# Layer 1 of a two-layer attention kernel: P scaled, split in two 16-bit parts and transposed by DMA; values in two 16-bit parts

## The chip, the cores and the metric

The kernel runs on one core of a Trainium2 chip. A core has TensorE (PE), VectorE (DVE), ScalarE (ACT), GpSimd (POOL) and SyncE (SP), which run side by side, each in its own order, and meet at semaphores; 16 DMA engines move data. The metric is the device time of one execution in microseconds.

## The reference

Two layers on x of shape 2 x 192 x 64 x 64. Layer 0 is an attention of four heads behind a depthwise convolution; the change leaves it alone. Layer 1, cut to what matters:

```python
xf = x.reshape(b, c, h * w).transpose(0, 2, 1)          # group norm before, 4096 tokens, 192 channels
xn = layer_norm(xf) * ln_w + ln_b
Q, K, V = xn @ Wq.T, xn @ Wk.T, xn @ Wv.T
S = einsum('bnd,bmd->bnm', Q, K)                        # 4096 x 4096 an image
attn = e1/(e1+e2) * softmax(S) + e2/(e1+e2) * relu(S)**2
out = einsum('bnm,bmd->bnd', attn, V) + x
```

The second term has no normalisation, so S is squared as it is: that is why products are made from two parts of a value (a rounded high part and the rest).

## The kernel before

`layer1` takes the images one after the other. A prologue per image (group norm, layer norm, projections, stores and loads of q and k) ends with `kst` (keys, two parts), `q_scratch` in HBM and `v_hl`: the values of all 4096 tokens as [high | low], 384 columns, in float32r (F32R), a 4-byte type.

Then comes the attention loop: 32 rows (`RB`) of 128 queries. In a row the 4096 scores stand in 4 chunks of 1024 (`NQ`, index c), two PSUM buffers `ps_s`; P is turned and weighed in 8 groups of 512 keys (`NG`). All five engines have the loop written out by hand as slots: in slot t TensorE makes the scores of row t+1, ScalarE and VectorE finish P of row t, and TensorE weighs row t-1. Odd and even rows use buffer s = 0 or 1.

- TensorE, `score_half` (L1277): five matmuls of 512 columns, half a chunk. `transpose_group` (L1288): four transposes of P into one of three PSUM buffers `ps_t`. `weigh_group` (L1298): four pairs, `at_hi` with 384 columns of `v_hl` and `at_lo` with 192, added up in `ps_o`. `turn_output` (L1307) turns the finished row back to channels by tokens. A score half waits (semaphore `exped`) until ScalarE has read the buffer two chunks before.
- VectorE, `maximum` (L1476, L1478): the chunk's row maximum and the bias of its exp; behind the fourth `nbmin` (L1481). `coefficients` (L1487 to L1493), which wait for ScalarE's `factors`. `combine` (L1500): P = P x coef + square, 128x1024, both inputs in SBUF (`gp` and `vb` or `rn`). `low_group` (L1505): `at_lo` = `ps_t` - `at_hi`, 128x512. `copy_output` (L1510, L1512) and `add_output` (L1519).
- ScalarE, `relu` (L1120), `exp_piece` (L1131), `square` (L1125), `factors` (L1137) and `high_group` (L1143): `at_hi`, the rounded copy of `ps_t`.
- SP issues `load_q`, `load_res` and `store` of a row (L1020, L1025, L1030). GpSimd does nothing in the loop.

In layer 0 GpSimd subtracts too: `lo` = `u` - `hi` (L389), behind VectorE's cast (L641), beside its convolution (L592).

## Time and profile before

| what | value |
|---|---|
| median of 3 runs | 3994.99 us |
| lowest, highest | 3993.24, 3997.37 us |
| the profiled execution | 3993.2 us |
| its span, first to last instruction | 3991.4 us |
| mean granted TensorE clock | 0.957 |
| TensorE, VectorE, ScalarE, GpSimd busy | 3574.1, 2171.5, 2221.6, 342.2 us |

Busy time is a mean over stages with different limits. The attention loops of layer 1 lie at about 2320 to 3060 us (image 0) and 3248 to 3991 us (image 1) of the span; layer 0 ends before 2100. A timeline row gives the start and the length of an instruction or of several of one kind (xN), and in brackets how long the engine had been idle before and what released it. Instructions of one engine overlap by about 0.1 us, so an instruction's share of its engine's time is read from one start to the next. A row of engines by stretch gives the stretch, its length, and each engine's busy time with its number of instructions.

### The profile page before, as it was taken

The numbers are of one execution on the slowest core, as the hardware profiler recorded it, in microseconds if no ns is written. First come the engines' busy times: TensorE is split into PE (matmuls) and PEld (weight loads), VectorE is DVE, ScalarE is ACT, GpSimd is POOL, SyncE is SP. The second block draws the span as 40 slices with busy tenths as digits, with TensorE's granted clock in tenths as the row PEclk, the third lists the DMA queues.
The fourth block names the chain that finished last, engine by engine and source line by source line (L and its number), as shares of the span: only waits on it lengthen the run. The fifth ranks groups of instructions, "written<-read, shape, count | busy, mean of one in ns | idle before, by whom it ended". The sixth has DMA issues, their size and how long they took to land. (4 is left out here: it accounts for less than half of the span.)

```text
span 3991.4 us, 53719 instructions
## 1 busy us (share of the span) xinstructions
PE 3574.1 (90%) x18516; PEld 1946.7 (49%) x18516; DVE 2171.5 (54%) x2749; ACT 2221.6 (56%) x2690; POOL 342.2 (9%) x124
## 2 busy tenths in 40 slices
PE   1269999999999999999997679999998669999999
PEld 0022322223222232222222358888886248888888
DVE  4744157331565234652014457777776447777777
ACT  0036555465555655556661257777773147777776
POOL 0212012020110201101001200000000300000000
PEclk9579999999999999999998889999999789999999
DMA  6221112121121211102003520101012350010100
GB/s 178 55 56 32 40 35 66 36 43 41 33 55 36 50 37 37 50 18 51 3 5 93 162 81 25 29 24 30 24 29 70 107 148 24 25 28 24 30 24 18
DMA packets 166881, 194.73 MB, mean 49 GB/s; under 512 B 28802, under 2 KB 105474, under 8 KB 164994
## 3 DMA queue, kind: packets, MB, share of 16 engines
q1 hardware_dynamic: 166724, 192.65, 18.8%
q8 instruction: 97, 1.59, 0.2%
q14 instruction: 60, 0.49, 0.0%
HBM read 106.01 MB, written 50.92 MB: 39 GB/s over the span
## 5 line engine op out<-in xcount | busy, mean ns | idle before, releaser
L413 ACT ACTIVATE prob<-ps_s,cur 128x1024 f32<-128x1024 f32 x1024 | 1085.5, 1111 | 794.4 <-PE ps_s L493 792.8
L506 PE MATMUL ps_a<-prob,vt 128*64 128x512 f32 x4096 | 997.6, 608 | 0.0
L1277 PE MATMUL ps_s<-kst,qs 128*128 128x512 f32 x2560 | 690.2, 401 | 47.6 <-DMA qs<-q_scratch 34.7
L1298 PE MATMUL ps_o<-v_hl,at_hi 128*128 128x384 f32 x2048 | 646.3, 372 | 2.3 <-DVE at_lo L1505 2.3
L487 PE MATMUL ps_s<-q_a,k_a 128*128 128x512 f16 x2048 | 537.6, 385 | 10.1 <-issue 5.1
L1298 PE MATMUL ps_o<-v_hl,at_lo 128*128 128x192 f32 x2048 | 513.1, 251 | 0.0
L1277 PEld LDWEIGHTS ps_s<-kst,qs 128*128 128x128 f32 x2560 | 448.3, 190 | 120.4 <-issue 37.2
L506 PEld LDWEIGHTS ps_a<-prob,vt 128*64 128x64 f32 x4096 | 249.6, 136 | 412.9 <-issue 412.2
L1505 DVE TENSOR_TENSOR at_lo<-ps_t,at_hi 128x512 fp32r<-128x512 f32 x512 | 351.6, 687 | 155.8 <-ACT at_hi L1143 146.9
L487 PEld LDWEIGHTS ps_s<-q_a,k_a 128*128 128x128 f16 x2048 | 142.9, 98 | 520.5 <-ACT prob L413 412.6
L1476 DVE TENSOR_REDUCE nmx<-ps_s 128x1 f32<-128x1024 f32 x256 | 311.5, 1217 | 153.9 <-PE ps_s L1277 153.9
L1298 PEld LDWEIGHTS ps_o<-v_hl,at_lo 128*128 128x128 f32 x2048 | 391.3, 191 | 4.9
L1298 PEld LDWEIGHTS ps_o<-v_hl,at_hi 128*128 128x128 f32 x2048 | 385.8, 188 | 8.8 <-DVE at_lo L1505 4.0
L1288 PE MATMUL ps_t<-ident,gp 128*128 128x128 f32 x2048 | 299.4, 273 | 22.7 <-DVE at_lo L1505 22.7
L1143 ACT ACTIVATE at_hi<-ps_t 128x512 fp32r<-128x512 f32 x512 | 294.1, 603 | 28.5 <-PE ps_t L1288 28.5
L1131 ACT ACTIVATE gp<-ps_s,nbias,mix 128x1024 f32<-128x1024 f32 x256 | 308.7, 1206 | 0.0
L666 DVE RECIPROCAL rden<-ps_h 128x512 f32<-128x512 f32 x32 | 107.5, 3358 | 340.6 <-PE ps_h L461 340.6
L592 DVE SCALAR_TENSOR_TENSOR qk<-pad,vec,qk 112x2048 f32<-112x2048 f32 x128 | 290.3, 2346 | 0.0
L1288 PEld LDWEIGHTS ps_t<-ident,gp 128*128 128x128 f32 x2048 | 241.5, 140 | 78.1 <-issue 32.4
L575 DVE TENSOR_SCALAR pad<-ps_h,vec 112x512 f32<-112x512 f32 x96 | 72.2, 752 | 333.7 <-PE ps_h L430 333.7
L1120 ACT ACTIVATE vb<-ps_s 128x1024 f32<-128x1024 f32 x128 | 131.4, 1027 | 217.3 <-DVE nmx L1476 217.3
L1120 ACT ACTIVATE rn<-ps_s 128x1024 f32<-128x1024 f32 x128 | 131.4, 1027 | 184.3 <-DVE nmx L1476 184.3
(143 smaller groups left out, 2902.9 us busy)
## 6 DMA issues: line engine op xcount, KB each, us to landing
z<-z_scratch SPq DMA_DIRECT2D x96, 384.0 KB, 3.6
q_scratch<-qst SPq DMA_DIRECT2D x64, 384.0 KB, 5.0
qs<-q_scratch SPq DMA_DIRECT2D x64, 384.0 KB, 3.8
sq<-rn_scratch SPq DMA_DIRECT2D x16, 768.0 KB, 10.2
gn_x<-in_x SPq DMA_DIRECT2D x4, 1536.0 KB, 18.4
z_scratch<-gn_x SPq DMA_DIRECT2D x4, 1536.0 KB, 11.6
q_a<-hi SPq DMA_DIRECT2D x64, 96.0 KB, 2.3
o_scratch<-o_s SPq DMA_DIRECT2D x64, 96.0 KB, 1.9
```

Source lines behind the costliest of these rows:

```text
L413: act.activation(prob[:, a % PR, :], ps_s[:, a % 2, :], ACT.Exp, bias=cur[:, slot:slot + 1], scale=1.0 / SPLIT).then_inc(exped, 1)
L487: pe.matmul(ps_s[:, n % 2, h * CH:(h + 1) * CH], k_a[:, slot, m * P:(m + 1) * P], q_a[:, slot, cols], start=True, stop=False)
L506: ins = pe.matmul(ps_a[h * HALF:(h + 1) * HALF, j % 2, :], vt[:, slot, m, :], prob[:, a % PR, h * CH:(h + 1) * CH], start=(m == 0), stop=( ...
L592: ins = dve.scalar_tensor_tensor(out=out, in0=src, scalar=vec[0:KR, slot, 1 + tap:2 + tap], in1=out, op0=ALU.mult, op1=ALU.add)
L1120: act.activation(sqr[s][:, cols], ps_s[:, c % 2, :], ACT.Relu).then_inc(relued, 1)
L1131: act.activation(prob[s][:, c * QB:(c + 1) * QB], ps_s[:, c % 2, :], ACT.Exp, bias=nbias[:, s, c:c + 1], scale=mix[:, 6:7], accum_out=sums ...
L1143: act.activation(at_hi[:, j % 4, :], ps_t[:, turn_bank(at), :], ACT.Copy).then_inc(hi_made, 1)
L1277: ins = pe.matmul(ps_s[:, c % 2, h * CH:(h + 1) * CH], qs[:, s, qt, :], kst[:, ktile, cols], start=(t == 0), stop=(t == len(terms) - 1))
L1288: ins = pe.transpose(ps_t[:, turn_bank(at), m * P:(m + 1) * P], prob[s][:, cols], ident[:, :])
L1298: ins = pe.matmul(ps_o[:, 0:wide], a[:, j % 4, m * P:(m + 1) * P], v_hl[:, kt, 0:wide], start=(kt == 0 and t == 0), stop=(kt == KT - 1 and ...
L1476: dve.tensor_reduce(nmx[:, c:c + 1], ps_s[:, c % 2, :], AX_X, ALU.max, negate=True).then_inc(mx_op, 1)
L1505: dve.tensor_tensor(at_lo[:, j % 4, :], ps_t[:, turn_bank(at), :], at_hi[:, j % 4, :].bitcast(F32), ALU.subtract).then_inc(t_free, 1)
```

## The change

P is scaled by powers that keep it inside the 16-bit range: relu by `GAIN`, square by `inv` (one over the row's largest score, at least one), the coefficients by the same factor, and the output by `back` and per channel by `unscale`. `v_hl`, scaled by `scale_v` through `wv`, is F16. A few instructions before the first image (`reach_step`) work out `scale_v` and `unscale`.

P's high part is no longer made from a transposed copy in PSUM. VectorE casts each combined chunk to `p_hi` (`high`, F16), GpSimd subtracts to `p_lo` (`lows`), and SP issues one DMA transpose for each part and chunk (`turn_chunk`), eight a row, into `at_hi` and `at_lo`, which now hold a whole row twice. ScalarE's `high_group`, VectorE's `low_group` and TensorE's `transpose_group` are gone. SP's loop is written out without a hardware loop.

```diff
-        v_hl = sb("v_hl", [P, KT, 2 * C], F32R)
+        v_hl = sb("v_hl", [P, KT, 2 * C], F16)
-        at_hi = sb("at_hi", [P, 4, GR * P], F32R)
-        at_lo = sb("at_lo", [P, 4, GR * P], F32R)
+        at_hi = sb("at_hi", [P, 2, KT, P], F16)
+        at_lo = sb("at_lo", [P, 2, KT, P], F16)
+        p_hi = sb("p_hi", [P, N], F16)
+        p_lo = sb("p_lo", [P, N], F16)
...
+                    def turn_chunk(row, s, c, first=False):
+                        cols = slice(c * QB, (c + 1) * QB)
+                        if not first:
+                            sp.wait_ge(w_done, NG * (RB * b + row - 2) + 2 * c + 2)
+                        sp.wait_ge(hi_made, NQ * (RB * b + row) + c + 1)
+                        sp.dma_start_transpose(at_hi[:, s, c * KC:(c + 1) * KC, :], p_hi[:, cols]).then_inc(turned[c], 16)
+                        sp.wait_ge(lo_made, NQ * (RB * b + row) + c + 1)
+                        sp.dma_start_transpose(at_lo[:, s, c * KC:(c + 1) * KC, :], p_lo[:, cols]).then_inc(turned[c], 16)
+
+                    def slot(t, s, first=False, more_q=True):
+                        for c in range(NQ):
+                            turn_chunk(t, s, c, first and t < 2 and b == 0)
+                            if c == 0:
+                                if more_q:
+                                    load_q(t + 2, s)
+                                if not first:
+                                    store(t - 2, s)
+                                load_res(t, s, first and b == 0)
...
+                    def lows(row, s):
+                        for c in range(NQ):
+                            cols = slice(c * QB, (c + 1) * QB)
+                            pool.wait_ge(hi_made, NQ * (RB * b + row) + c + 1)
+                            pool.tensor_tensor(p_lo[:, cols], prob[s][:, cols], p_hi[:, cols], ALU.subtract).then_inc(lo_made, 1)
+
+                    with pool.Fori(0, RB // 2) as r:
+                        lows(2 * r, 0)
+                        lows(2 * r + 1, 1)
...
-                        act.activation(sqr[s][:, cols], ps_s[:, c % 2, :], ACT.Relu).then_inc(relued, 1)
+                        act.activation(sqr[s][:, cols], ps_s[:, c % 2, :], ACT.Relu, scale=GAIN).then_inc(relued, 1)
-                        act.activation(sqr[s][:, cols], sqr[s][:, cols], ACT.Square).then_inc(squared, 1)
-
+                        act.activation(sqr[s][:, cols], sqr[s][:, cols], ACT.Square, scale=inv[:, s:s + 1]).then_inc(squared, 1)
+
+                    def exp_piece(row, s, c, first=False):
                         act.wait_ge(mx_op, MX * (RB * b + row) + 2 * c + 2)
-                        if at is not None:
-                            act.wait_ge(t_full, turn(b, row - 2, at) + 1)
+                        if not first:
+                            act.wait_ge(lo_made, NQ * (RB * b + row - 2) + c + 1)
...
+                    def slot(t, s, new=True, first=False, older=False):
+
+                        exp_piece(t, s, NQ - 1, older)
+                        factors(t, s)
+                        square(t, s, 0)
+                        square(t, s, 1)
+                        if new:
+                            relu(t + 1, 1 - s, 0, first)
+                        square(t, s, 2)
+                        if new:
+                            exp_piece(t + 1, 1 - s, 0, first)
+                        square(t, s, 3)
+                        if new:
+                            for c in range(1, NQ):
+                                relu(t + 1, 1 - s, c, first)
+                                if c < NQ - 1:
+                                    exp_piece(t + 1, 1 - s, c, first)
...
-                    def transpose_group(row, s, j, at):
-                        pe.wait_ge(t_free, turn(b, row, at) + 1)
-                        if j % 2 == 0:
-                            pe.wait_ge(p_made, NQ * (RB * b + row) + j // 2 + 1)
+                    def weigh_group(row, s, u, first=False):
+                        if u == 0 and not first:
+                            pe.wait_ge(ob_made, RB * b + row - 1)
+                        if u % 2 == 0:
+                            pe.wait_ge(turned[u // 2], 32 * (RB * b + row + 1))
                         for m in range(GR):
-                            cols = slice((j * GR + m) * P, (j * GR + m + 1) * P)
-                            ins = pe.transpose(ps_t[:, turn_bank(at), m * P:(m + 1) * P], prob[s][:, cols], ident[:, :])
-                        ins.then_inc(t_full, 1)
-
-                    def weigh_group(row, j, at):
-                        pe.wait_ge(t_free, TR + turn(b, row, at) + 1)
-                        if j == 0:
-                            pe.wait_ge(ob_made, RB * b + row + 1)
-                        for m in range(GR):
-                            kt = j * GR + m
+                            kt = u * GR + m
                             for t, (a, wide) in enumerate(((at_hi, 2 * C), (at_lo, C))):
-                                ins = pe.matmul(ps_o[:, 0:wide], a[:, j % 4, m * P:(m + 1) * P], v_hl[:, kt, 0:wide],
+                                ins = pe.matmul(ps_o[:, s * CH:s * CH + wide], a[:, s, kt, :], v_hl[:, kt, 0:wide],
                                                 start=(kt == 0 and t == 0), stop=(kt == KT - 1 and t == 1))
                         ins.then_inc(w_done, 1)
...
-                    def slot(t, s, j, q, new):
-
-                        for g in range(2):
-                            transpose_group(t - 1, 1 - s, g, place(q, g))
+                    def slot(t, s, j, new=True, out=True, first=False):
+
                         for u in range(NG):
                             if new:
                                 score_half(t + 1, 1 - s, j, u)
-                            if u == 0 and q >= 1:
-                                turn_output(t - 2, 2)
-                            if u + 2 < NG:
-                                transpose_group(t - 1, 1 - s, u + 2, place(q, u + 2))
-                            weigh_group(t - 1, u, place(q, u))
+                            if u == 1 and out:
+                                turn_output(t - 2, s, first)
+                            weigh_group(t - 1, 1 - s, u, first)
...
+                reach_step(dve.scalar_tensor_tensor(out=g[:, :, 0:C], in0=wv[:, :, :], scalar=-1.0, in1=wv[:, :, :],
+                                                    op0=ALU.mult, op1=ALU.max))
+                for t in range(CT):
+                    reach_step(dve.tensor_scalar(g[:, t, 0:C], g[:, t, 0:C], reach[:, t, 2:3], None, ALU.mult))
+                dve.wait_ge(reach_full, 1)
+                reach_step(dve.tensor_scalar(scale_v[:, :], ps_t[0:CP, 0, 0:C], 1e-30, C / SPAN, ALU.max, ALU.mult))
...
+                for t in range(CT):
+                    dve.tensor_tensor(wv[:, t, :], wv[:, t, :], scale_v[:, :], ALU.mult)
+                    ins = dve.tensor_scalar(unscale[:, t:t + 1], ps_t[0:CP, 1, t * 8:t * 8 + 1], 1e-30, C / SPAN, ALU.max, ALU.mult)
+                reach_step(ins)
...
+                            dve.wait_ge(mx_op, at + 2 * NQ + 1)
+                            dve.tensor_scalar(m1[:, s:s + 1], nbmin[:, s:s + 1], mix[:, 7:8], -1.0, ALU.mult, ALU.min).then_inc(mx_op, 1)
+                            dve.wait_ge(mx_op, at + 2 * NQ + 2)
+                            dve.reciprocal(inv[:, s:s + 1], m1[:, s:s + 1]).then_inc(mx_op, 1)
...
+                        dve.scalar_tensor_tensor(out=back[:, s:s + 1], in0=m1[:, s:s + 1], scalar=1.0 / (GAIN * GAIN),
+                                                 in1=m1[:, s:s + 1], op0=ALU.mult, op1=ALU.mult).then_inc(c_op, 1)
+                        dve.wait_ge(c_op, at + 3)
+                        dve.tensor_tensor(total[:, :], total[:, :], back[:, s:s + 1], ALU.mult).then_inc(c_op, 1)
+                        dve.wait_ge(c_op, at + 4)
                         dve.reciprocal(total[:, :], total[:, :]).then_inc(c_op, 1)
-                        dve.wait_ge(c_op, at + 3)
+                        dve.wait_ge(c_op, at + 5)
                         dve.tensor_scalar(coef[:, s, :], fac[:, s, :], total[:, 0:1], mix[:, 4:5], ALU.mult, ALU.mult).then_inc(c_op, 1)
-                        dve.wait_ge(c_op, at + 4)
+                        dve.wait_ge(c_op, at + 6)
...
-                    def low_group(row, j, at):
-                        dve.wait_ge(hi_made, NG * (RB * b + row) + j + 1)
-                        dve.tensor_tensor(at_lo[:, j % 4, :], ps_t[:, turn_bank(at), :], at_hi[:, j % 4, :].bitcast(F32),
-                                          ALU.subtract).then_inc(t_free, 1)
+                    def high(row, s, c, first=False):
+
+                        cols = slice(c * QB, (c + 1) * QB)
+                        dve.wait_ge(p_made, NQ * (RB * b + row) + c + 1)
+                        if not first:
+                            dve.wait_ge(turned[c], 32 * (RB * b + row))
+                        dve.tensor_copy(p_hi[:, cols], prob[s][:, cols]).then_inc(hi_made, 1)
+                    def copy_output(row, s):
+                        dve.wait_ge(w_done, NG * (RB * b + row) + NG)
+                        dve.tensor_scalar(ob_lo[:, :], ps_o[:, s * CH + C:s * CH + 2 * C], back[:, s:s + 1], None,
+                                          ALU.mult).then_inc(ob_lo_made, 1)
-                        dve.tensor_tensor(ob[:, :], ps_o[:, 0:C], ob_lo[:, :], ALU.add).then_inc(ob_made, 1)
+                        dve.scalar_tensor_tensor(out=ob[:, :], in0=ps_o[:, s * CH:s * CH + C], scalar=back[:, s:s + 1],
+                                                 in1=ob_lo[:, :], op0=ALU.mult, op1=ALU.add).then_inc(ob_made, 1)
...
-                        dve.tensor_tensor(ot[:, s, :, :], ps_t[0:CP, turn_bank(at), 0:CT * P].rearrange("p (t n) -> p t n", t=CT),
-                                          res[:, s, :, :], ALU.add).then_inc(t_free, 1)
+                        for t in range(CT):
+                            ins = dve.scalar_tensor_tensor(out=ot[:, s, t, :], in0=ps_t[0:CP, s, t * P:(t + 1) * P],
+                                                           scalar=unscale[:, t:t + 1], in1=res[:, s, t, :],
+                                                           op0=ALU.mult, op1=ALU.add)
+                        ins.then_inc(ot_made, 1)
+
+                    def slot(t, s, j, new=True, out=True, first=False):
+
+                        if out:
+                            copy_output(t - 2, s)
+                        coefficients(t, s)
+                        combine(t, s, 0)
+                        high(t, s, 0, first)
+                        if out:
+                            add_output(t - 2, s, j)
                         if new:
                             maximum(t + 1, 1 - s, 0)
-                        if old:
-                            combine(t, s, 1)
-                        low(3)
-                        if old:
-                            combine(t, s, 2)
-                        low(4)
+                        combine(t, s, 1)
+                        high(t, s, 1, first)
                         if new:
                             maximum(t + 1, 1 - s, 1)
-                        if old:
-                            combine(t, s, 3)
-                        low(5)
-                        low(6)
+                        combine(t, s, 2)
+                        high(t, s, 2, first)
+                        combine(t, s, 3)
+                        high(t, s, 3, first)
                         if new:
                             maximum(t + 1, 1 - s, 2)
-                        low(7)
-                        if new:
                             maximum(t + 1, 1 - s, 3)
```

TensorE, image 0, one step of the loop with a new row to score: scores of one half, the turn of P, a weigh group. Before:

```order
L1277 MATMUL ps_s<-kst,qs 128x512 x5
L1288 MATMUL ps_t<-ident,gp 128x128 x4
L1298 MATMUL ps_o<-v_hl,at_hi 128x384
L1298 MATMUL ps_o<-v_hl,at_lo 128x192
L1298 MATMUL ps_o<-v_hl,at_hi 128x384
L1298 MATMUL ps_o<-v_hl,at_lo 128x192
L1298 MATMUL ps_o<-v_hl,at_hi 128x384
```

After:

```order
L1287 MATMUL ps_s<-kst,qs 128x512 x5
L1300 MATMUL ps_o<-v_hl,at_hi 128x384
L1300 MATMUL ps_o<-v_hl,at_lo 128x192
L1300 MATMUL ps_o<-v_hl,at_hi 128x384
L1300 MATMUL ps_o<-v_hl,at_lo 128x192
L1300 MATMUL ps_o<-v_hl,at_hi 128x384
```

The four transposes of a step have gone; scores and weigh groups stand in the same order and number.

VectorE, the middle of an early row (combines, maxima, and before the low parts; `gp` is P, `rn` the square). Before:

```order
L1500 SCALAR_TENSOR_TENSOR gp<-gp,coef,rn 128x1024 [waits squared]
L1505 TENSOR_TENSOR at_lo<-ps_t,at_hi 128x512 [waits hi_made]
L1500 SCALAR_TENSOR_TENSOR gp<-gp,coef,rn 128x1024 [waits squared]
L1505 TENSOR_TENSOR at_lo<-ps_t,at_hi 128x512 [waits hi_made]
L1476 TENSOR_REDUCE nmx<-ps_s 128x1 [waits s_full]
L1478 TENSOR_SCALAR nbias<-nmx,mix 128x1 [waits mx_op]
L1500 SCALAR_TENSOR_TENSOR gp<-gp,coef,rn 128x1024 [waits squared]
L1505 TENSOR_TENSOR at_lo<-ps_t,at_hi 128x512 [waits hi_made] x2
L1476 TENSOR_REDUCE nmx<-ps_s 128x1 [waits s_full]
L1478 TENSOR_SCALAR nbias<-nmx,mix 128x1 [waits mx_op]
L1505 TENSOR_TENSOR at_lo<-ps_t,at_hi 128x512 [waits hi_made]
```

After:

```order
L1531 SCALAR_TENSOR_TENSOR gp<-gp,coef,rn 128x1024 [waits squared]
L1540 CAST p_hi<-gp 128x1024 [waits turned1,p_made]
L1499 TENSOR_REDUCE nmx<-ps_s 128x1 [waits s_full]
L1501 TENSOR_SCALAR nbias<-nmx,mix 128x1 [waits mx_op]
L1531 SCALAR_TENSOR_TENSOR gp<-gp,coef,rn 128x1024 [waits squared]
L1540 CAST p_hi<-gp 128x1024 [waits turned2,p_made]
L1531 SCALAR_TENSOR_TENSOR gp<-gp,coef,rn 128x1024 [waits squared]
L1540 CAST p_hi<-gp 128x1024 [waits turned3,p_made]
L1499 TENSOR_REDUCE nmx<-ps_s 128x1 [waits s_full]
L1501 TENSOR_SCALAR nbias<-nmx,mix 128x1 [waits mx_op]
L1499 TENSOR_REDUCE nmx<-ps_s 128x1 [waits s_full]
L1501 TENSOR_SCALAR nbias<-nmx,mix 128x1 [waits mx_op]
```

Each combine is now followed by a cast to `p_hi`, combines 2 and 3 stand together, and the maxima of chunks 2 and 3 have moved behind them to the row's end.

SP, the last rows of an image before, and one row of image 0 after. Before:

```order
L1020 DMA qs<-q_scratch 128x6x128 [waits s_full]
L1025 DMA res<-res_scratch 96x2x128 [waits ot_stored]
L1030 DMA out<-ot 96x2x128 [waits t_free]
L1025 DMA res<-res_scratch 96x2x128 [waits ot_out,ot_stored]
L1030 DMA out<-ot 96x2x128 [waits t_free]
```

After:

```order
L1042 DMA_TRANSPOSE at_hi<-p_hi 128x8x128 [waits hi_made,w_done]
L1044 DMA_TRANSPOSE at_lo<-p_lo 128x8x128 [waits lo_made1]
L1023 DMA qs<-q_scratch 128x6x128 [waits s_full]
L1034 DMA out<-ot 96x2x128 [waits ot_made]
L1029 DMA res<-res_scratch 96x2x128 [waits ot_made]
L1042 DMA_TRANSPOSE at_hi<-p_hi 128x8x128 [waits hi_made,w_done]
L1044 DMA_TRANSPOSE at_lo<-p_lo 128x8x128 [waits lo_made1]
```

The load of qs, the store and the load of res stand behind the first chunk's two transposes, and six more transposes follow.

## Rows read from the trace of the kernel before

**Rows 1.** engines by stretch: PE, PEld, DVE, ACT, POOL busy us, clock, DMA share, GB/s
```profile
2700.00:2926.00 226.00, 222.67 (x1382) 200.35 (x1381) 174.11 (x282) 167.32 (x251) 0.00 (x0) 1.00 0.09 26
```

**Rows 2.** timeline of SP's queue: start, us, instruction; stores of two rows
```profile
2423.74 0.34 SPq L1030 DMA_DIRECT2D out<-ot  x1
...
2446.35 0.34 SPq L1030 DMA_DIRECT2D out<-ot  x1
```

**Rows 3.** timeline of TensorE, one step of a row
```profile
2408.25 1.33 PE L1277 MATMUL ps_s<-kst,qs 128*128 128x512 f32 x5
2409.41 0.60 PE L1288 MATMUL ps_t<-ident,gp 128*128 128x128 f32 x4
2409.77 0.42 PE L1298 MATMUL ps_o<-v_hl,at_hi 128*128 128x384 f32 x1
...
2410.97 1.33 PE L1277 MATMUL ps_s<-kst,qs 128*128 128x512 f32 x5
```

**Rows 4.** timeline of VectorE in the same row
```profile
2419.44 0.36 DVE L1510 COPY ob_lo<-ps_o 128x192 f32<-128x192 f32 x1 [0.40 <-issue]
...
2421.55 0.16 DVE L1487 TENSOR_TENSOR part<-fac,sums 128x4 f32<-128x4 f32 x1 [0.68 <-ACT fac L1137]
...
2422.55 0.69 DVE L1505 TENSOR_TENSOR at_lo<-ps_t,at_hi 128x512 fp32r<-128x512 f32 x1
...
2425.29 1.21 DVE L1476 TENSOR_REDUCE nmx<-ps_s 128x1 f32<-128x1024 f32 x1
...
2426.67 1.27 DVE L1500 SCALAR_TENSOR_TENSOR gp<-gp,coef,vb 128x1024 f32<-128x1024 f32 x1
```

**Rows 5.** timeline, layer 0: cast, VectorE beside GpSimd
```profile
646.58 0.69 DVE L641 CAST hi<-u 112x1024 f16<-112x1024 f32 x1
...
647.19 8.75 DVE L592 SCALAR_TENSOR_TENSOR vv<-pad,vec,vv 112x2048 f32<-112x2048 f32 x3
...
647.36 4.17 POOL L389 TENSOR_TENSOR lo<-u,hi 112x1024 f16<-112x1024 f32 x1 [7.58 <-DVE hi L641]
```

**Rows 6.** timeline of ScalarE: relu, exp, factors
```profile
2418.64 1.03 ACT L1120 ACTIVATE vb<-ps_s 128x1024 f32<-128x1024 f32 x1 [0.53 <-DVE nmx L1476]
...
2420.03 1.21 ACT L1131 ACTIVATE gp<-ps_s,nbias,mix 128x1024 f32<-128x1024 f32 x1
...
2421.22 0.30 ACT L1137 ACTIVATE fac<-nbias,nbmin 128x4 f32<-128x4 f32 x1
```

**Rows 7.** one line's instructions: ns min/median/max
```profile
L389 POOL TENSOR_TENSOR lo<-u,hi x32: 2127/3148/4183, 191.2 to 1853.1; 112x1024 f16<-112x1024 f32 x32
```

**Rows 8.** timeline, layer 1 before the loop: two-element mode beside GpSimd
```profile
2236.30 0.87 DVE L1467 TENSOR_SCALAR gp<-gp,pvec 96x512 f32<-96x512 f32 x2
...
2238.34 2.36 POOL L1076 TENSOR_TENSOR xs<-gp,xs 96x1024 fp32r<-96x1024 f32 x1 [14.40 <-ACT xs L1095]
...
2238.42 2.96 DVE L1467 TENSOR_SCALAR gp<-gp,pvec 96x512 f32<-96x512 f32 x2
```

**Rows 9.** timeline, layer 1 before the loop: an operand in PSUM beside GpSimd
```profile
3179.98 2.35 POOL L1076 TENSOR_TENSOR xs<-gp,xs 96x1024 fp32r<-96x1024 f32 x1 [6.79 <-ACT xs L1095]
3180.92 1.22 DVE L1450 TENSOR_TENSOR qst<-ps_s,qst 96x1024 fp32r<-96x1024 f32 x1 [2.10 <-ACT qst L1102]
```

**Rows 10.** timeline, layer 0's start: a copy of one column beside GpSimd
```profile
71.42 1.65 POOL L393 TENSOR_TENSOR root<-root,half_t 128x8 f32<-128x8 f32 x1 [0.32 <-DVE root L679]
71.59 0.15 DVE L655 COPY cur<-tabs 128x1 f32<-128x1 f32 x1
```

**Rows 11.** timeline: TensorE's first score of image 0, SP's first load of image 1
```profile
2320.65 6.89 PE L1277 MATMUL ps_s<-kst,qs 128*128 128x512 f32 x20 [18.85 <-DMA qs<-q_scratch]
...
3061.76 0.32 SPq L971 DMA_DIRECT2D o_buf<-o_scratch  x1
```

**Rows 12.** timeline of TensorE, image 1's run-up: after an idle
```profile
3271.54 7.57 PE L1277 MATMUL ps_s<-kst,qs 128*128 128x512 f32 x20 [3.24 <-ACT gp L1131]
```

**Rows 13.** engines by stretch, columns as in Rows 1: 2 us of that run-up
```profile
3272.00:3274.00 2.00, 2.00 (x6) 1.52 (x6) 1.97 (x3) 1.39 (x3) 0.00 (x0) 0.50 0.00 0
```

225 lines of the change are left out of this document (95 added, 130 removed).

## The prediction, made before the changed kernel ran

> **What bounds the kernel now.** The change touches layer 1 alone, in its attention loop, so I read that stage. The table of engines by stretch [rows 1], over ten of its rows, has TensorE busy 222.67 of 226 us at the full granted clock; VectorE has 174.11, ScalarE 167.32, GpSimd nothing, and the DMA engines are 9% busy. TensorE is the bound. Two successive stores of one row's output are 22.61 us apart [rows 2]; that is the period of a row, 32 to an image. The order of TensorE's work inside a row shows where it goes [rows 3]: a score half (five matmuls) holds it from 2408.25 to 2409.41 = 1.16 us, four transposes of P to 2409.77 = 0.36, four pairs of P x V to 2410.97 = 1.20, so 2.72 a step. Eight steps make 21.8; the output's turn and a short wait at the row's end are the rest.
>
> **TensorE after.** The 32 transposes go: 8 x 0.36 = 2.9 us. P x V keeps its columns (576 a pair), now in 16 bits. A pair took about 0.29; 576 columns at 2.4 GHz are 0.24. So a group costs 0.96 to 1.15, and I take 1.0. A row then needs 8 x (1.16 + 1.0) + 0.3 = 17.6 us: TensorE alone would give 5 us a row. The rest of this working asks what is late next.
>
> **VectorE's own work after**, as start-to-start times in today's rows [rows 4]:
> - output copy 0.36 (2419.44) and sum, as long again: 0.74 from start to start;
> - the coefficients: today 2421.55 to 2422.55 = 1.00, with two more tiny instructions of 0.17 = 1.34;
> - four maxima with their bias: 2425.29 to 2426.67 = 1.38 each, 5.5; plus nbmin, m1 and inv behind the last, 0.7;
> - four combines at 1.27, each now followed by a cast that waits for it, so 1.30 each, 5.2;
> - four casts f32 to f16. Layer 0 has the same instruction on 112 partitions: 0.69, and 0.61 from start to start [rows 5]; 2.4 together;
> - the output sum, now in two pieces: 0.45.
> Together 16.4. The eight low parts (0.60 each, 4.8) are gone; that is what pays for casts and small steps. ScalarE loses eight copies of P and needs relu (1.03), exp with its read (2420.03 to 2421.22 = 1.19) and a square like the relu, four times each: about 12.6 [rows 6]. Neither engine's sum reaches 17.6.
>
> **The wait for ScalarE.** In the new order VectorE does the maxima 2 and 3 back to back at the end of a row. From the end of maximum 2, ScalarE has relu, exp, relu, exp and the factors before it: 2 x (1.03 + 1.19) + 0.3, less 0.2 where one starts before the last is through = 4.5 us [rows 6]. VectorE has bias, maximum 3, its small steps and the output copy: 1.4 + 0.7 + 0.74 + 0.1 = 2.95. So it stands about 1.6 before the coefficients. Queued behind that wait is the whole of its row.
>
> **GpSimd and the lock.** The low part of P moves to GpSimd: four subtractions of 128x1024 a row. Layer 0 has this form (f16 from f32 and f16); the shortest took 2127 ns [rows 7]. The same place shows what it does beside VectorE [rows 5]: the subtraction asked for at 647.36 took 4.17, because a VectorE instruction with two SBUF inputs had started at 647.19 (2.35 alone); and three of those took 8.75, where 3 x 2.26 = 6.8 was due, so one of them stood 1.9. Whichever starts first keeps the other out to its end. A single-input instruction that runs at two elements a cycle is shut out too: two of L1467 take 0.87 (2236.30); the next two, at 2238.42, took 2.96, since a GpSimd subtraction had started at 2238.34 [rows 8]. VectorE instructions that read PSUM are not: L1450 took its usual 1.22 inside a GpSimd subtraction [rows 9]. So combines and casts are locked out, maxima and output steps are not.
>
> Now the row in its new order. Cast 0 starts low 0 (2.13); VectorE has the output sum and maximum 0 (1.8) to do, then combine 1 stands 0.35. Cast 1 starts low 1; only maximum 1 (1.38) lies beside it: combine 2 stands 0.8. Behind cast 2 comes combine 3 at once; as in layer 0 it starts before the semaphore reaches GpSimd, low 2 waits for it, and cast 3 then stands a whole 2.13. Low 3 lies beside maxima 2 and 3 and the output copy: nothing. Together 3.3 us. **Sum: 16.4 + 1.6 + 3.3 + 0.3 (loop branches and single waits, 0.15 today) = 21.6 us a row**, against 22.61. TensorE waits 4 us of it.
>
> Small instructions of one element per partition I take as free of the lock: a copy of 128x1 at 71.59 took 0.15 while GpSimd ran from 71.42 for 1.65 [rows 10]. The Trainium skill (SBUF — State Buffer, practical consequences) says that copies and tensor_scalar can all enter the two-port modes and contend; by it the bias of maximum 2 would stand 1 us behind low 3, and rival B below is that case.
>
> **The transposes by DMA.** No row shows one. Eight a row, 256 KB each, 2 MB in all. Today's traffic of a row (qs, res and out, 576 KB in 1152 pieces of 512 B, 72 per engine) keeps an engine 0.09 x 22.6 = 2.0 us busy [rows 1], 28 ns a piece. A transpose of 128x1024 cut at its 128-column blocks has 1024 pieces of 256 B, 64 per engine: 14 ns each if bytes count, 28 if pieces do, so 0.9 to 1.8 us. Nearest in kind is the piece; I take 1.4. With today's 2.0 a row needs 9 to 16.5 us of the DMA engines, hidden under 21.6. Its latency is hidden too: chunk 0 of a row is needed 15 us after its cast, and at_hi and at_lo have two slots. The lower bound of its cost is therefore nothing. SP's queue has eight transposes with two semaphores each; behind them stand the load of qs (needed 13 us later), the store and the load of res. It holds while one transpose costs SP or the DMA engines under (21.6 - 1.5) / 8 = 2.5 us.
>
> The Trainium skill gives two prices. DMA: Bandwidth & Descriptors (Latency and other measured facts) has 261 GB/s for transposes, an estimate of 1.0 us each. The same page (on HWDGE) has 262,144 sequencer cycles for 8,192 tiles in earlier generations, 32 a tile; at the SyncEngine's 1.2 GHz (Trainium Kernel Development and Optimization) 64 tiles would hold SP 1.7 us, 14 us a row as an estimate. No row here shows either; by both the sum stays as it is.
>
> **The whole.** An image's attention lasts from its first score at 2320.65 to the next image's first load at 3061.76, 741.1 us [rows 11]: 31 periods of 22.6 and 40.5 of run-up and run-off. After: 31 x 21.6 + 39 = 708.6, since the last row now passes a transpose but loses the copies. That is 32.5 less, 65 for both images. The new steps on wv before the first chunk lie mostly beside loads; 2 us. **3993.2 - 63 = 3930 us**, for a profiled execution that stood 1.8 under the median, so the same number serves for the median.
>
> **Rivals.**
> - **B, small steps are locked too.** Then the bias of maximum 2 stands 1 us behind low 3 and the row takes 22.2: 31 x 22.2 + 39 = 727, 27 less for both images, 3968; a little more overhead and it is 3990, no change.
> - **C, the casts escape the lock.** For: L1467 is one case. Then lows 0 to 2 fit behind maxima, VectorE's row is its 16.4 plus waits for exp and scores, 19.9 in all: 31 x 19.9 + 30 = 647, 3805.
> - **D, the transposes bound** (slower). From 2.5 us a transpose, in SP's queue or the DMA engines, they set the row; every 0.1 us adds 0.8. At 3.0 the row is 24 + 1.5 = 25.5: 31 x 25.5 + 45 = 836, 95 more an image, 4183. For: a write of 16 rows' elements is far finer than any row shows. Against: 2.5 us for 64 pieces an engine is 39 ns, above the 28 of twice the size.
> - **E, the clock falls** (slower). TensorE would idle 2.3 us at a row's end and 1.5 in its middle. After an idle of 3.24 us, before 3271.54 [rows 12], the clock stood at 0.50, 1.2 GHz [rows 13]. If it fell so at every row, the first two steps would take twice as long, maximum 0 would wait, and the row be 23.3: 761 an image, 4035. The idle is shorter than the one that did it.
> - **The change isn't made**: the instruction order shows DMA_TRANSPOSE and no TensorE transpose of P, so this has no share.
>
> **Chances.** Forecast (own range 3895 to 3960) 0.53; B 0.12; C 0.11; D 0.14; E 0.10. Faster by over 0.2% (3987; about what a measurement of this kernel tells from no change): forecast, C and half of B, with a small loss to the edges, 0.68. Within 0.2%: the other half of B and the mild end of D, 0.08. Slower: 0.24. The range takes in C and E, and leaves out D's upper part and what lies below C: 3800 to 4045.
>
> **What would show it.** Right: row period 21 to 22; VectorE gaps of about 2 us before a cast with GpSimd busy; GpSimd subtractions of 2.1 and some of 3.4; TensorE busy about 80% of the stage at 1.00. Wrong: subtractions never above 2.2 and no standing casts (C); SP's transposes back to back and P x V waiting for them (D); a granted clock below 0.9 in the stage (E); nbias at over 1 us (B).

## Result: 3896 us, 2.5% faster, and the profile after

The changed kernel takes 3895.98 us (median; 3895.58 to 3897.90) against 3996.09 (3993.24 to 3997.37): a ratio of 0.9751, 95% interval 0.9734 to 0.9768. The forecast was 3930 us, two thirds of the gain. The measured time lies inside the stated range (3800 to 4045 us) and at the lower edge of the forecast's own (3895 to 3960).

Engines over the stretch of [rows 1], same columns:

```profile
2700.00:2926.00 226.00, 194.91 (x1143) 134.23 (x1142) 200.97 (x314) 141.46 (x187) 102.64 (x43) 1.00 0.64 130
```

TensorE is down from 222.67 to 194.91 us of 226, VectorE is up from 174.11 to 200.97, GpSimd does 102.64 where it did nothing, and the DMA share went from 0.09 to 0.64. The clock is 1.00. The chain that ended last, as shares of the span, now runs through VectorE's combinations (L1531) and maxima (L1499):

```profile
DVE 22%; issue 9%; PE 5%; ACT 4%; SPq 2%; POOL 2%; DMA 1%; DVEq 0%; ACTq 0%; POOLq 0%
DVE gp L1531 10%; DVE nmx L1499 7%; ACT gp L1155 3%; PE ps_s L1233 2%; DVE p_hi L1540 1%; SPq L1009 1%; SPq L1000 1%; POOL xg L1085 1%; DVE ot L1557 1%; PE ps_s L1287 1%; PE ps_o L1300 1%; PE ps_s L1254 1%; DVE coef L1524 0%; DMA rn<-r_scratch 0%; DMA q_scratch<-qst 0%
```

TensorE in that stretch (start, us). A step has lost its transposes [rows 3]:

```profile
2602.54 1.39 PE L1287 MATMUL ps_s<-kst,qs 128*128 128x512 f32 x5
2603.78 0.34 PE L1300 MATMUL ps_o<-v_hl,at_hi 128*128 128x384 f16 x1
...
2604.72 1.39 PE L1287 MATMUL ps_s<-kst,qs 128*128 128x512 f32 x5
...
2608.39 1.43 PE L1287 MATMUL ps_s<-kst,qs 128*128 128x512 f32 x5 [1.28 <-ACT gp L1155]
...
2619.01 1.43 PE L1287 MATMUL ps_s<-kst,qs 128*128 128x512 f32 x5 [1.47 <-ACT gp L1155]
```

From score half to score half it is 2604.72 - 2602.54 = 2.18 us (was 2.72), and twice a row TensorE now stands, 1.28 and 1.47 us, until ScalarE's exponential has freed a score bank. It is no longer the bound. VectorE and GpSimd over a row (start, us; in brackets the idle time before it and what ended it):

```profile
2606.05 0.21 DVE L1501 TENSOR_SCALAR nbias<-nmx,mix 128x1 f32<-128x1 f32 x1
...
2610.66 0.16 DVE L1514 TENSOR_TENSOR part<-fac,sums 128x4 f32<-128x4 f32 x1 [1.56 <-ACT fac L1161]
...
2611.92 1.28 DVE L1531 SCALAR_TENSOR_TENSOR gp<-gp,coef,rn 128x1024 f32<-128x1024 f32 x1
2613.33 0.69 DVE L1540 CAST p_hi<-gp 128x1024 f16<-128x1024 f32 x1
...
2615.84 1.48 DVE L1531 SCALAR_TENSOR_TENSOR gp<-gp,coef,rn 128x1024 f32<-128x1024 f32 x1
...
2619.35 2.00 DVE L1531 SCALAR_TENSOR_TENSOR gp<-gp,coef,rn 128x1024 f32<-128x1024 f32 x1
2621.39 0.69 DVE L1540 CAST p_hi<-gp 128x1024 f16<-128x1024 f32 x1
2622.00 1.28 DVE L1531 SCALAR_TENSOR_TENSOR gp<-gp,coef,rn 128x1024 f32<-128x1024 f32 x1
2623.31 2.52 DVE L1540 CAST p_hi<-gp 128x1024 f16<-128x1024 f32 x1
...
2629.58 0.42 DVE L1544 TENSOR_SCALAR ob_lo<-ps_o,back 128x192 f32<-128x192 f32 x1 [0.35 <-issue]
...
2631.52 0.16 DVE L1514 TENSOR_TENSOR part<-fac,sums 128x4 f32<-128x4 f32 x1 [1.07 <-ACT fac L1161]
```

```profile
2604.97 2.14 POOL L1097 TENSOR_TENSOR p_lo<-gp,p_hi 128x1024 f16<-128x1024 f32 x1 [0.63 <-DVE p_hi L1540]
...
2618.13 2.14 POOL L1097 TENSOR_TENSOR p_lo<-gp,p_hi 128x1024 f16<-128x1024 f32 x1 [1.89 <-DVE p_hi L1540]
2622.16 3.11 POOL L1097 TENSOR_TENSOR p_lo<-gp,p_hi 128x1024 f16<-128x1024 f32 x1 [1.89 <-DVE p_hi L1540]
```

The combination takes 1.27 alone and the cast 0.69. The combination at 2615.84 took 1.48, the one at 2619.35 2.00, the cast at 2623.31 2.52: each has a GpSimd subtraction beside it and ends after it. Below, such an instruction is said to stand. GpSimd's subtraction at 2622.16 took 3.11 in place of 2.13, since the combination of 2622.00 was first. In the next row VectorE is idle in two pieces, 0.35 us with no other engine to release it and 1.07 for ScalarE's factors; the two kinds of row take turns (20.86 and 20.99 us). The DMA transposes, on SyncE's queue (ns min/median/max) with their time to landing:

```profile
L1042 SPq DMA_TRANSPOSE at_hi<-p_hi x256: 1230/1282/1957, 2340.7 to 3880.8; - x128
...
DMA to landing us min/median/max: 3.1/3.3/5.6
```

### The profile page after: what moved, and what is told of

Its sections match the earlier page's. It is cut to its first block and busy times, and to the rows that moved or that the text cites. A ratio compares the mean times of both kernels' runs of the same rounds, so it can differ in the third digit from the quotient of the medians.

```text
span 3894.2 us, 48213 instructions
## 1 busy us (share of the span) xinstructions
PE 3310.9 (85%) x16480; PEld 1472.9 (38%) x16480; DVE 2261.5 (58%) x2824; ACT 1979.0 (51%) x2178; POOL 956.6 (25%) x380
## 5 line engine op out<-in xcount | busy, mean ns | idle before, releaser
L1287 PE MATMUL ps_s<-kst,qs 128*128 128x512 f32 x2560 | 722.3, 414 | 221.8 <-ACT gp L1155 186.9
L1097 POOL TENSOR_TENSOR p_lo<-gp,p_hi 128x1024 f16<-128x1024 f32 x256 | 614.5, 2400 | 803.4 <-DVE p_hi L1540 803.4
L1300 PE MATMUL ps_o<-v_hl,at_hi 128*128 128x384 f16 x2048 | 552.8, 331 | 8.5 <-DMA at_lo<-p_lo 8.5
L1300 PE MATMUL ps_o<-v_hl,at_lo 128*128 128x192 f16 x2048 | 506.0, 248 | 0.0
L1499 DVE TENSOR_REDUCE nmx<-ps_s 128x1 f32<-128x1024 f32 x256 | 310.7, 1214 | 48.8 <-PE ps_s L1287 48.8
L1540 DVE CAST p_hi<-gp 128x1024 f16<-128x1024 f32 x256 | 301.4, 1177 | 13.7
L390 POOL TENSOR_TENSOR sq<-qk 112x1024 f32<-112x1024 f32 x32 | 59.6, 1894 | 992.8 <-DVE qk L598 992.8
L1300 PEld LDWEIGHTS ps_o<-v_hl,at_hi 128*128 128x128 f16 x2048 | 201.0, 98 | 228.0 <-issue 129.0
L436 PE MATMUL ps_h<-z,w 96*112 96x512 f32 x384 | 186.8, 620 | 39.4 <-DMA z<-z_scratch 39.3
L499 PE MATMUL ps_s<-q_b,k_b 16*128 16x512 f16 x2048 | 203.5, 387 | 0.0
```

Source lines behind the costliest of these rows:

```text
L1097: pool.tensor_tensor(p_lo[:, cols], prob[s][:, cols], p_hi[:, cols], ALU.subtract).then_inc(lo_made, 1)
L1287: ins = pe.matmul(ps_s[:, c % 2, h * CH:(h + 1) * CH], qs[:, s, qt, :], kst[:, ktile, cols], start=(t == 0), stop=(t == len(terms) - 1))
L1300: ins = pe.matmul(ps_o[:, s * CH:s * CH + wide], a[:, s, kt, :], v_hl[:, kt, 0:wide], start=(kt == 0 and t == 0), stop=(kt == KT - 1 and t ...
L1499: dve.tensor_reduce(nmx[:, c:c + 1], ps_s[:, c % 2, :], AX_X, ALU.max, negate=True).then_inc(mx_op, 1)
L1540: dve.tensor_copy(p_hi[:, cols], prob[s][:, cols]).then_inc(hi_made, 1)
```

## The experiments

Theory A, from the profile: a row is now VectorE's: about 16.6 us of its own, 1.3 of waiting for ScalarE's factors (1.56 at 2610.66, 1.07 at 2631.52), 0.2 for the gap of 0.35 in every second row, and 2.8 in which GpSimd's subtractions keep it out. The expectations below have 16.4 and 1.56 in place of 16.6 and 1.3; they took the longer wait for both rows. Theory B: it is still TensorE's. Theory C: it is set by the transposes, on SyncE's queue or the DMA engines. "Row" in this table is the time from the first to the last row's coefficients in image 0, divided by 31. In the kernel before, that mean takes in a first row of 16.2 us; its steady row is 22.59 us (22.55 and 22.63 in turn), that of the kernel after 20.92. The kernels that leave work out are marked * (half_lows half of the low parts, the others the last product of a score).

| kernel | row, us | time, us | ratio to before (95%) |
|---|---|---|---|
| before | 22.37 | 3996 | 1 |
| after | 20.95 | 3896 | 0.9751 (0.9734 to 0.9768) |
| half_lows * | 20.37 | 3857 | 0.9659 (0.9643 to 0.9675) |
| twice_lows | 24.98 | 4162 | 1.0414 (1.0397 to 1.0432) |
| max2_early | 20.45 | 3864 | 0.9675 (0.9658 to 0.9691) |
| max0_early | 23.84 | 4084 | 1.0225 (1.0208 to 1.0242) |
| both_early | 20.35 (image 1: 21.20) | 3896 | 0.9753 (0.9737 to 0.9769) |
| max2_fill | 20.05 | 3844 | 0.9626 (0.9613 to 0.9639) |
| best_order | 17.51 | 3693 | 0.9245 (0.9230 to 0.9260) |
| four_terms * | 20.89 | 3893 | 0.9749 (0.9733 to 0.9766) |
| best_four * | 16.71 | 3642 | 0.9110 (0.9095 to 0.9126) |
| before_four * | 21.70 | 3950 | 0.9889 (0.9872 to 0.9905) |
| turn12 | 21.19 | 3916 | 0.9803 (0.9787 to 0.9819) |
| best_turn12 | 18.56 | 3770 | 0.9435 (0.9419 to 0.9451) |

### How much GpSimd's work costs VectorE: half_lows and twice_lows

```diff
@@ lows, half_lows
-                            cols = slice(c * QB, (c + 1) * QB)
+                            cols = slice(c * QB, c * QB + CH)
@@ lows, twice_lows
+                            pool.tensor_tensor(p_lo[:, cols], prob[s][:, cols], p_hi[:, cols], ALU.subtract).then_inc(lo_once, 1)
+                            pool.wait_ge(lo_once, NQ * (RB * b + row) + c + 1)
                             pool.tensor_tensor(p_lo[:, cols], prob[s][:, cols], p_hi[:, cols], ALU.subtract).then_inc(lo_made, 1)
```

half_lows also clears `p_lo` once, before the first image; the low parts that are not formed stay zero.

> Leaves out: GpSimd forms the low part of half the columns only (128x512 per chunk in place of 128x1024; the other half of the low part stays zero), so each of its four subtractions a row should fall from 2.13 to about 1.05 us. Theory A (the row is VectorE's: its own 16.4 us, 1.56 us of waiting for ScalarE's factors and 2.75 us in which VectorE and GpSimd keep each other out): the stalls fall by half or more, the row goes from 20.92 to 19.5 us (19.1 to 20.0), the kernel from 3896 to about 3808 us (3785 to 3840). Theory B (TensorE still sets the row, 86% busy) and theory C (the transposes by DMA or SyncE's queue set it, which are the same eight as before): row and kernel stay, 3885 to 3900 us.

> The kernel after the change with each of GpSimd's subtractions made twice in a row (8 x 2.13 us a row in place of 4; the result is the same). Theory A: VectorE is kept out twice as often: of its four pairs of combination and cast each meets a subtraction that runs, the stalls go from 2.75 us a row to 7 to 9 us, the row from 20.92 to 23.5 to 27.5 us, most likely 26, the kernel to 4210 us (4055 to 4305). Rival (GpSimd's busy time, 8.5 of 20.9 us before the doubling and 17 after, is felt only through the low parts' later arrival, a row ahead of their use): 3896 to 3910 us.

Measured: 3857 us, 17 above the expected range, and 4162 us, inside it. B and C, and the rival for twice_lows, are out: the row follows GpSimd's work although nothing waits long for the low parts. Doubling gives 4.0 us a row, where I took 5 for likeliest. VectorE in twice_lows, from the middle of one row to the middle of the next:

```profile
2599.86 2.00 DVE L1534 SCALAR_TENSOR_TENSOR gp<-gp,coef,vb 128x1024 f32<-128x1024 f32 x1
2601.90 2.52 DVE L1543 CAST p_hi<-gp 128x1024 f16<-128x1024 f32 x1
2604.34 1.27 DVE L1534 SCALAR_TENSOR_TENSOR gp<-gp,coef,vb 128x1024 f32<-128x1024 f32 x1
2605.64 2.50 DVE L1543 CAST p_hi<-gp 128x1024 f16<-128x1024 f32 x1
...
2613.92 0.53 DVE L1517 TENSOR_TENSOR part<-fac,sums 128x4 f32<-128x4 f32 x1 [1.56 <-ACT fac L1164]
...
2621.16 2.52 DVE L1543 CAST p_hi<-gp 128x1024 f16<-128x1024 f32 x1
```

GpSimd's:

```profile
2600.86 3.00 POOL L1100 TENSOR_TENSOR p_lo<-gp,p_hi 128x1024 f16<-128x1024 f32 x1
...
2612.28 2.14 POOL L1100 TENSOR_TENSOR p_lo<-gp,p_hi 128x1024 f16<-128x1024 f32 x1
```

Casts 1, 2 and 3 stand 1.8 us each, combination 2 0.7 and the first instruction of the coefficients 0.4: 6.6 us a row in place of 2.8, and the difference is nearly the whole of the row's 4.0.

Halving gave 0.6 us a row, where I expected 1.4. Of VectorE's stands one of 0.8 us is left there (cast 3), and another wait appears. TensorE, half_lows:

```profile
2609.01 1.42 PE L1290 MATMUL ps_s<-kst,qs 128*128 128x512 f32 x5 [2.25 <-ACT gp L1158]
```

and VectorE waits 1.70 us, to 2616.99, for the scores behind them before its last maximum. VectorE and TensorE stand in a ring: exponential 0 frees the bank for the scores of chunk 2, then come chunk 3's, maximum 3, the factors, the coefficients, combination 0, cast 0, maximum 0, and exponential 0 of the next row. With most of the stalls out, a steady row takes 20.0 to 20.3 us; five of them take 21.5 to 21.7, and each of the five has a stretch of TensorE at half its granted clock (of this more under max2_fill), which makes the mean of 20.4. That the ring is what holds the other rows at 20 was argued from the order of the waits here; best_order, which opens it, tests it. The prediction left it out.

### Which work stands beside the subtraction: max2_early, max0_early, both_early

The same instructions in another order on VectorE, nothing else:

```diff
@@ vector engine's slot, max2_early
                         high(t, s, 2, first)
+                        if new:
+                            maximum(t + 1, 1 - s, 2)
                         combine(t, s, 3)
                         high(t, s, 3, first)
                         if new:
-                            maximum(t + 1, 1 - s, 2)
                             maximum(t + 1, 1 - s, 3)
@@ max0_early (both_early is the two together)
                             copy_output(t - 2, s)
+                        if new:
+                            maximum(t + 1, 1 - s, 0)
                         coefficients(t, s)
...
-                        if new:
-                            maximum(t + 1, 1 - s, 0)
                         combine(t, s, 1)
```

> Same work in another order on VectorE alone: the maximum over chunk 2 of the next row stands between cast 2 and combination 3, no longer behind cast 3. Theory A: GpSimd's subtraction of chunk 2 then runs beside a maximum, which reads PSUM and isn't kept out; cast 3 loses its stall of 1.83 us, the row falls from 20.92 to about 19.6 us (19.1 to 20.2), the kernel to about 3815 us (3785 to 3850). Theory B and C: nothing that TensorE or the transposes do changes, and each finds its input at most 1.4 us earlier or later; 3880 to 3905 us.

> Same work in another order on VectorE alone: the maximum over chunk 0 of the next row stands ahead of the coefficients, where VectorE waits 1.56 us a row for ScalarE, and no longer between cast 0 and combination 1. Theory A: the wait is filled (1.4 us gained), but now combination 1 and cast 1 stand right behind cast 0, where GpSimd's subtraction runs: up to 2.13 us of stall for combination 1 in place of 0.20 us, and every later cast then is behind a subtraction that came late. The row gets longer, 22 to 24.3 us, the kernel 3965 to 4105 us, most likely 4060. Rival A2 (VectorE sets the row, but the stalls with GpSimd are no part of it: it would wait for the squares at these places anyway): the row falls by the filled wait to about 19.4 us, 3800 us. Theories B and C: 3880 to 3905 us.

> Same work: maximum 0 ahead of the coefficients, as in the run that took 4084 us, and maximum 2 between cast 2 and combination 3, as in the run that took 3864 us. Theory A (stalls with GpSimd follow from which work stands behind a cast): with maximum 2 back between, cast 3 and combination 3 lose most of their stall, but combination 1 and cast 1 still stand right behind cast 0 (one cast of 2.5 us a row): row 19.3 to 20.8 us, most likely 20.0, kernel 3840 us (3795 to 3890). Rival (effects of the two moves add): 3896 + 188 - 32 = 4052 us.

Measured: 3864 us (14 above the expected range), 4084 (inside it) and 3896 (6 above it, 56 above the likeliest value). Moving one maximum into a wait made the kernel 4.8% slower, as A said and A2, B and C did not. VectorE in max0_early:

```profile
2601.27 1.23 DVE L1499 TENSOR_REDUCE nmx<-ps_s 128x1 f32<-128x1024 f32 x1 [2.94 <-PE ps_s L1287]
...
2606.45 1.27 DVE L1531 SCALAR_TENSOR_TENSOR gp<-gp,coef,rn 128x1024 f32<-128x1024 f32 x1
2607.76 2.52 DVE L1540 CAST p_hi<-gp 128x1024 f16<-128x1024 f32 x1
...
2611.57 1.98 DVE L1531 SCALAR_TENSOR_TENSOR gp<-gp,coef,rn 128x1024 f32<-128x1024 f32 x1
...
2615.51 2.50 DVE L1540 CAST p_hi<-gp 128x1024 f16<-128x1024 f32 x1
```

Cast 1 and cast 3 both take 2.5 us, 1.8 more than alone: no maximum lies beside the subtraction before them. The place is the one that A named, but I had put the stall on combination 1, which started first and stood for nothing; it is cast 1 behind it that stands. That makes 1.8 + 0.7 + 1.8 = 4.3 us a row in place of 2.8. The wait that the move was to fill came back as 2.94 us for TensorE's scores (in the next row 2.44 and a gap of 0.36): 16.6 + 4.3 + 2.9 = 23.8, the measured row. TensorE's own wait, and the engines by stretch right behind it (columns as in [rows 1]):

```profile
2613.71 1.45 PE L1287 MATMUL ps_s<-kst,qs 128*128 128x512 f32 x5 [2.58 <-ACT gp L1155]
```

```profile
2615.00:2619.00 4.00, 4.00 (x16) 2.64 (x16) 3.97 (x3) 0.00 (x0) 3.37 (x2) 0.57 1.08 203
```

After an idle of 2.58 us the granted clock is 0.57 over four microseconds: 1.2 GHz for most of them. Nearly every row of image 0 has such a stretch, and the mean over the image is 0.92. How much of the 2.94 us that makes was not separated. max2_early shows the cast cured (2616.70, 2620.72: 0.69 each) and the ring again at 20.4; here too the clock fell in one row, after a wait of 2.33 us (2634.48), and not in the one before, after 2.25 (2614.31). The next fall of that image came after a wait of 2.25 (2736.54), with waits of 2.33 before it that left the clock at 1.00.

In both_early, image 0 has a row of 20.35, near the 20.0 that I expected, and image 1 one of 21.20 (657.3 us over 31 rows) with a mean clock of 0.96 in place of 0.99. TensorE's wait and the stretch behind it there:

```profile
3635.90 1.43 PE L1287 MATMUL ps_s<-kst,qs 128*128 128x512 f32 x5 [2.61 <-ACT gp L1155]
```

```profile
3637.00:3641.00 4.00, 4.00 (x16) 2.55 (x15) 3.35 (x4) 2.21 (x3) 2.11 (x2) 0.57 1.09 205
```

After a wait of 2.61 us the clock was down; in image 0 the waits are 2.39 and 2.47, and it stayed at 1.00 there. But the length of the wait doesn't settle it: image 1 goes in threes, with a fall after 2.61 and after 2.58 us and none after the longest:

```profile
3594.82 1.43 PE L1287 MATMUL ps_s<-kst,qs 128*128 128x512 f32 x5 [2.78 <-ACT gp L1155]
```

Why the two images differ is open.

### What the clock costs: max2_fill

```diff
@@ score_half, max2_fill: on top of max2_early
+                        if u == 4:
+                            for i in range(8):
+                                pe.matmul(ps_t[:, s, CH // 2:CH], qs[:, s, i % 3, :], kst[:, i % 3, 0:CH // 2], start=True, stop=True)
                         if h == 0:
```

> The order that took 3864 us (maximum 2 early), with eight matmuls of 256 columns added to TensorE's row right ahead of its wait for exponential 0, into columns of PSUM that nobody reads: some 0.9 us that lie in a wait of 2.3 us. In that order the granted clock is 0.98 over the attention stages; it is 0.50 for some 3.7 us after the wait of 2.33 us ending at 2634.48 and stays 1.00 after the one of 2.25 us ending at 2614.31. Theory (the falls of the clock cost part of the row): the wait is shorter, the clock stays at 1.00, and the row of 20.45 us loses the 0.2 to 0.5 us that the falls add: kernel 3845 us (3832 to 3856), with more work on TensorE. Rival (the falls lie inside TensorE's slack and cost nothing; or the added work delays the ring): 3860 to 3890 us.

Measured: 3844.44 us (3838.82 to 3845.95), 20 us less than max2_early (3861.59 to 3870.36), with more work on TensorE. Its wait and image 0 as a whole, after and then before the filler:

```profile
2603.49 1.20 PE L1280 MATMUL ps_t<-kst,qs 128*128 128x256 f32 x8
2605.97 1.42 PE L1290 MATMUL ps_s<-kst,qs 128*128 128x512 f32 x5 [1.28 <-ACT gp L1155]
```

```profile
2340.00:2960.00 620.00, 574.34 (x3465) 411.86 (x3465) 526.47 (x890) 403.65 (x527) 265.16 (x124) 1.00 0.67 134
```

```profile
2340.00:2960.00 620.00, 547.17 (x3157) 381.48 (x3156) 515.57 (x877) 395.22 (x515) 258.76 (x121) 0.98 0.65 130
```

The wait is 1.28 us in place of 2.25, the clock 1.00 in place of 0.98, the row 20.05 in place of 20.45. The falls did cost part of the row; what is left, 20.05 us, is what the ring holds with the clock at full speed.

### TensorE: four_terms, before_four, best_four

```diff
@@ score_half, in each of the three
-                        terms = [(0, 0), (3, 0), (1, 1), (4, 1), (2, 2)]
+                        terms = [(0, 0), (3, 0), (1, 1), (4, 1)]
```

> Leaves out: the last of the five products that make up a score (the low by low one), so each half of a score takes four matmuls in place of five: 0.23 us less eight times a row, 1.84 us of TensorE a row. Theory B (TensorE sets the row): the row falls from 20.92 to 19.1 us, the kernel to 3782 us plus what the edges give (3770 to 3800). Theory A: TensorE has 2.9 us idle a row already; the scores come a little earlier, the row falls by at most 0.3 us, 3875 to 3897 us. Theory C: no change, 3890 to 3900 us.

> The kernel before, without the last of the five products of a score (0.23 us less eight times a row, 1.84 us of TensorE): what relief of TensorE alone is worth in the old loop. If TensorE alone set its row of 22.61 us, 20.8 us and 3994 - 114 = 3880 us. Its VectorE is nearly as long (it copies half of the transposed groups out of PSUM too), so I expect part of that only: 21.4 us (20.8 to 22.2), kernel 3920 us (3880 to 3970). Rival (the old row was never TensorE's): 3990 us.

> The order of the 3693 us run without the fifth product of a score (1.84 us of TensorE a row less), which gave 3 us in the loop whose row took 20.9. Theory: in this order TensorE sets the row (busy 400.00 of 400 us in the second image), VectorE is next with 16.4 us of its own and 0.6 us of stalls: the row falls from 17.5 to 16.6 to 17.4 us, the kernel to 3665 us (3635 to 3688). Rival (VectorE and TensorE are bound by one another in a ring, as in the other orders): 3688 to 3695 us.

Taking 1.84 us a row off TensorE is worth 0.06 us in the kernel after (3 us in all), 0.67 in the kernel before, 0.81 in the order of the next section. So B is out for the kernel after, and the forecast's first step, that TensorE bounds the kernel before, was true for the first 0.7 us only (steady row 22.59 to 21.91). In before_four TensorE is busy

```profile
2700.00:2926.00 226.00, 213.84 (x1339) 189.24 (x1339) 178.38 (x293) 173.04 (x262) 0.00 (x0) 1.00 0.09 26
```

95%, and it waits for VectorE's low parts of P, 18.5 us in 400 where it was 6.0. The bound behind it stood 3% away. By this run a change that only took work off TensorE would have gained little; this one also took the eight low parts of 0.60 us off VectorE.

### The transposes: turn12 and best_turn12

```diff
@@ turn_chunk, turn12: each high part once more, to a spare tile
                         sp.dma_start_transpose(at_hi[:, s, c * KC:(c + 1) * KC, :], p_hi[:, cols]).then_inc(turned[c], 16)
-                        sp.wait_ge(lo_made, NQ * (RB * b + row) + c + 1)
+                        n = NQ * (RB * b + row) + c
+                        if n:
+                            sp.wait_ge(x_in, 16 * n)
+                        sp.dma_start_transpose(at_x[:, :, :], p_hi[:, cols]).then_inc(x_in, 16)
+                        sp.wait_ge(lo_made, n + 1)
@@ high
                             dve.wait_ge(turned[c], 32 * (RB * b + row))
+                            dve.wait_ge(x_in, 16 * (NQ * (RB * b + row - 1) + c + 1))
```

Both also make room for the spare tile, by letting two weights of the prologue (`wq`, `wk`) share their place with later tiles. best_turn12 is the same edit on best_order.

> Adds four transposes by DMA a row: each high part is transposed a second time, to a spare tile that nobody reads (12 in place of 8). Theory A: the DMA engines' share goes from 13.4 to 19.1 us of a row of 20.9, SyncE's queue from some 12 to 18 us, both still under the row: the low parts' transposes start up to 1.4 us later, which TensorE, a row behind, doesn't feel: 3890 to 3912 us. Theory C (transposes or their queue already set the row): 4 x 1.35 us more a row, 26 us, 4200 us or more.

> The order of the 3693 us run, whose row takes 17.5 us, with the four transposes a row that nobody reads added (12 in place of 8; they cost 20 us in all in the loop whose row took 20.9 us). From that run the DMA engines are busy 88% of 21.2 us = 18.7 us a row with twelve transposes. Theory: the transposes come to set the row here, because 18.7 us is over 17.5: 18.7 to 19.6 us a row, kernel 3693 + 62 x 1.2 to 2.1 = 3767 to 3823 us, most likely 3785. Rival (the DMA engines' share is no bound of its own, latency is all that counts and is hidden by a whole row): 3693 to 3725 us, the 20 us of before at most.

turn12: 3916 us, 0.24 us a row more, 4 us past what I allowed. C (4200) is out. VectorE's queue is enough to explain the rest: from combination 0 to cast 0 it is 1.50 us for 1.41 (2611.92 to 2613.33) with one more semaphore wait ahead of the cast. There are four a row, and the last takes its 0.09 out of cast 3's stand (2.43 for 2.52), which leaves 0.27. best_turn12: 3770 us, in the range of the theory. Both as a whole over their image 0:

```profile
2340.00:2980.00 640.00, 543.28 (x3141) 374.45 (x3140) 558.32 (x871) 390.03 (x512) 288.16 (x121) 0.99 0.90 176
```

```profile
2340.00:2900.00 560.00, 529.05 (x3129) 369.49 (x3130) 487.36 (x866) 395.90 (x512) 344.27 (x120) 1.00 1.01 198
```

In the second the DMA engines are busy all the time (1.01), and TensorE waits for the load of the next row's qs, 25 us in this stretch: the transposes set the row. SyncE's queue is full too, though. Two loads of qs in it:

```profile
2609.77 0.58 SPq L1026 DMA_DIRECT2D qs<-q_scratch  x1
...
2628.27 0.58 SPq L1026 DMA_DIRECT2D qs<-q_scratch  x1
```

In these 18.50 us stand twelve transposes and two more DMAs with gaps of at most 0.1 us. Whether the engines or the queue decides was not separated. A transpose costs the DMA engines (0.90 x 21.19 - 0.64 x 20.95) / 4 = 1.4 us, and (1.01 x 18.56 - 0.77 x 17.51) / 4 = 1.3 by the other pair. So rival D's mechanism exists; with eight transposes the DMA engines would decide in a row shorter than 8 x 1.4 + 2 = 13 us, an estimate from these and from the 2.0 us of the row's other traffic.

### The order that follows from A: best_order

```diff
@@ vector engine's slot
                             copy_output(t - 2, s)
+                        if new:
+                            maximum(t + 1, 1 - s, 0)
                         coefficients(t, s)
                         combine(t, s, 0)
                         high(t, s, 0, first)
+                        combine(t, s, 1)
+                        if new:
+                            maximum(t + 1, 1 - s, 1)
                         if out:
                             add_output(t - 2, s, j)
-                        if new:
-                            maximum(t + 1, 1 - s, 0)
-                        combine(t, s, 1)
                         high(t, s, 1, first)
-                        if new:
-                            maximum(t + 1, 1 - s, 1)
                         combine(t, s, 2)
+                        if new:
+                            maximum(t + 1, 1 - s, 2)
                         high(t, s, 2, first)
                         combine(t, s, 3)
+                        if new:
+                            maximum(t + 1, 1 - s, 3)
                         high(t, s, 3, first)
-                        if new:
-                            maximum(t + 1, 1 - s, 2)
-                            maximum(t + 1, 1 - s, 3)
```

> Same work, VectorE's order alone: maximum 0 of the next row ahead of the coefficients (in the wait for ScalarE), and maxima 1, 2 and 3 each between a combination and its cast, so that behind every cast but the first stands a combination whose lock is short or that finds GpSimd done. Runs so far: half the GpSimd work gave 3857 us and maximum 2 early gave 3864, both 20.3 us a row where theory A had 19.5: there TensorE waits 2.2 us once a row for exponential 0, which waits for maximum 0 (a ring of the scores of chunks 2 and 3, maximum 3, the factors, combination 0, maximum 0, exponential 0). Theory A with that ring: taking maximum 0 out from behind the coefficients opens the ring, the casts' stalls go, and TensorE's own 18.1 us (200.8 us busy in 226 us) set the row: 18.1 to 19.0 us, most likely 18.3, the kernel 3735 us (3715 to 3780). Rival (the ring isn't what holds the row at 20.3, but the transposes' latency or the queue on SyncE): the row stays at 20.0 to 20.4 us, 3840 to 3865 us.

Measured: 3692.91 us (3688.00 to 3694.05), 22 under the lower end of what I expected, 5.2% below the kernel after and 7.5% below the one before. The rival (3840 or more) is out. VectorE and GpSimd in it, and the engines over a stretch of image 1:

```profile
2602.58 0.69 DVE L1540 CAST p_hi<-gp 128x1024 f16<-128x1024 f32 x1
...
2603.19 1.28 DVE L1531 SCALAR_TENSOR_TENSOR gp<-gp,coef,rn 128x1024 f32<-128x1024 f32 x1
...
2603.35 3.11 POOL L1097 TENSOR_TENSOR p_lo<-gp,p_hi 128x1024 f16<-128x1024 f32 x1 [4.11 <-DVE p_hi L1540]
...
2604.39 1.22 DVE L1499 TENSOR_REDUCE nmx<-ps_s 128x1 f32<-128x1024 f32 x1
...
2606.28 0.73 DVE L1540 CAST p_hi<-gp 128x1024 f16<-128x1024 f32 x1
...
2609.51 1.25 DVE L1540 CAST p_hi<-gp 128x1024 f16<-128x1024 f32 x1
```

```profile
3240.00:3640.00 400.00, 400.00 (x2412) 283.74 (x2409) 367.72 (x663) 296.84 (x387) 262.42 (x92) 1.00 0.76 154
```

The combination that follows a cast starts before GpSimd has its semaphore, so it is GpSimd that stands (3.11 in place of 2.13, and it has the time), and a maximum covers the rest; cast 2 alone stands 0.56 us. The ring is open, since maximum 0 no longer waits for the coefficients. TensorE is busy 400.00 of 400 us: a row is 8 x 2.17 and the output's turn. Its steady row is 17.60 us (the 17.51 of the table has a shorter first and last), the 17.6 us which the prediction named as what TensorE alone would give.

## Why the prediction was right in direction and short in size

- **Row.** Forecast 21.6 us, measured 20.92 in the steady loop, from store to store as in [rows 2], and 20.95 as a mean over image 0. This is the main miss: 0.65 x 31 = 20 us an image. The sign named for a right forecast, a period of 21 to 22, was just missed; against the steady row before (22.59) the change takes 1.7 us off, where 1.0 was forecast. The 0.7 us are made of the smaller stalls (0.5), the shorter wait (0.3) and the smaller rest (0.1), less 0.2 by which VectorE's own work was put too low.
- **VectorE's own work.** 16.4 forecast; 20.92 - 1.32 (the wait) - 2.77 (the stalls) - 0.18 (an issue gap of 0.35 in every second row) = 16.65 measured, as the remainder. The cast in layer 0 was the right row for the new one (0.69).
- **The wait for ScalarE.** 1.6 forecast; 1.56 at 2610.66 and 1.07 at 2631.52, in turn, so 1.3 measured.
- **The stalls.** 0.35 + 0.8 + 2.13 = 3.3 forecast; 0.21 + 0.73 + 1.83 = 2.77 measured, each at the place named. The term was mis-sized, for cast 3 above all: I took the whole of GpSimd's 2.13, but the cast began (2623.31) only 1.96 before the subtraction ended (2625.27), and was through 0.56 after it, where it takes 0.69 alone; so it stood 1.83. The 0.3 for branches was 0.18.
- **TensorE.** Step 2.18 for a forecast of 2.16; need of a row 17.6, which best_order shows. It waits 1.28 + 1.47 = 2.8 us a row, not 4, and is busy 86% of the stage, not 80.
- **Edges.** An image's attention lasts from 2321.23 to 3016.10 = 694.9 us; less 31 x 20.95, 45.4 remain, where I put 39. It is not the last row: from its coefficients to the end are 29.1 us (2987.00 to 3016.10), 1.1 less than before (3031.52 to 3061.76). It is the first: before the change the second row's coefficients came 16.2 us after the first's (2338.13, 2354.30), and my 40.5 of edges held that saving of 6.4 us against 22.6; after it they come 20.7 us apart (2337.49, 2358.16). Why the first row was so short was not traced. Image 1 takes 692.6 (from 3201.59). Together the two images give -46.2 and -50.4, for -32.5 each in the forecast; run-up and prologue give -0.5.
- **Rival B, small steps locked**, is refuted in this kernel: the bias at 2606.05 took 0.21 inside the subtraction of 2604.97 to 2607.11. The Trainium skill (SBUF — State Buffer, practical consequences) says of tensor_scalar that it can contend when its operands meet certain conditions; the prediction dropped that condition. With one element per partition no run here shows any contention. But twice_lows shows that small size alone is no protection: the product of two 128x4 tiles in SBUF, at 2613.92, took 0.53 in place of 0.16 and ended with GpSimd's.
- **Rival C** is refuted: the cast stands (2.52).
- **Rival D** did not decide here: SyncE is held 1.24 to 1.28 us a transpose and the DMA engines 1.3 to 1.4, for 1.4 taken. The two prices of the Trainium skill (DMA: Bandwidth & Descriptors, Latency and other measured facts, and its sequencer cycles for HWDGE) were 1.0 us of the DMA engines and 1.7 us of SyncE by estimate, one below and one above what is measured.
- **Rival E**, the clock, did not happen in the steady rows (1.00), where the idle is in two pieces of 1.3 and 1.5 us; it did three times among the first rows, the last after an idle of 1.85 us (2429.8). It did in half_lows, max2_early, max0_early, image 1 of both_early and twice_lows, where TensorE stands for 2.1 to 4.9 us in one piece, and in four_terms, where it stands twice a row for 2.2 to 2.5. The mechanism exists; the steady row of this kernel doesn't meet it.
- **What was left out**: the ring through maximum 0, which is the floor right under the kernel after (20.05 at full clock, some 20.4 with the falls of the clock, against 20.95). Floor and falls together explain why taking away the stalls alone gave half or less of what their size promised.

## What to carry to other kernels

When work is moved to GpSimd, look at what VectorE does right behind the instruction that releases it. In this kernel combinations with two inputs in SBUF (2.00 for 1.27 us) and casts from SBUF (2.52 for 0.69) stood until the subtraction was over, and maxima that read PSUM did not (1.21). So the order of VectorE was worth more here than the length of GpSimd's instruction: one order cost 188 us and another gained 203, with the same instructions, where halving the subtractions gained 39. Price the second bound and the rings (a wait that closes over two rows) before counting on the whole of a stall, and if an engine must wait, see to it that TensorE's wait is short or filled.

## What the runs showed of the hardware that I had not expected

- Eight useless matmuls a row made the kernel 20 us faster (3864 to 3844), by keeping TensorE's clock at 1.00. The length of an idle alone does not tell whether the clock falls behind it: after 2.58 (max0_early) and 2.61 us (both_early) some 4 us stood mostly at 0.50, after 2.78 (both_early) they did not; after 2.25 us in max2_early they did once (2736.54), and mostly did not. What decides is not shown.
- four_terms left its row at 20.89, but the mean clock of image 0 fell to 0.94: work taken off an engine that waits can come back as a lower clock, and neither is seen in the time.
- One more semaphore wait ahead of a VectorE instruction, long fulfilled, costs about 0.09 us (turn12: 1.50 for 1.41).
- Instructions of a few elements are not all free beside GpSimd: 128x4 with two inputs in SBUF took 0.53 us in place of 0.16, 128x1 with one input its usual 0.21.
